# Three turned tiles that are turned again in the passes, from raw blocks, instead of being stored

## The reference

```python
h = relu(layernorm(x)); x = x + L0(h, adj)   # e = h with two small products; adj @ (adj.T @ e), normed, + h
h = relu(layernorm(x)); x = x + adj @ h                                    # pass 0
h = relu(layernorm(x)); x = x + chebyshev(h, adj, k = 3)                   # passes 1, 2, 3
h = relu(layernorm(x)); x = x + relu(d * ((adj + I) @ (d * (h @ W + b))))  # pass 4, d = (row sums + 1) ** -0.5
```

## Time and profile before

| | us |
|---|---|
| three runs | 1447.44, 1448.79, 1451.46 (median 1448.79) |
| profiled execution | 1448.4 |
| its span, first to last instruction | 1446.2 |
| turning stage, to the first product behind it | 551.4 |
| passes | 894.8 |

### The profile page before, as it was taken

The page is one execution under the profiler, slowest core; times in us unless marked ns, Lnnn a source line. Parts: engine busy times, 40 slices in busy tenths (PEclk is TensorE's granted clock), DMA queues, the critical chain, the costliest instruction groups (busy, mean ns, idle before and its releaser), DMA issues.

```text
span 1446.2 us, 18473 instructions
## 1 busy us (share of the span) xinstructions
PE 1419.2 (98%) x7601; PEld 600.5 (42%) x7601; DVE 491.8 (34%) x1082; ACT 399.3 (28%) x885; POOL 84.4 (6%) x67
## 2 busy tenths in 40 slices
PE   6999999999999999999999999999999999999998
PEld 3555555555555563333333333333333333333332
DVE  6694544544546533331132211011311121101044
ACT  2378778677776551000000000000000000000000
POOL 2210000000000038000000000000000000000000
PEclk9999999999999999999999999999999999999999
DMA  9999999999999998999996797899797948996998
GB/s 322 382 422 409 419 414 413 419 410 411 412 402 371 391 420 341 420 421 420 421 409 215 320 363 295 320 352 323 302 336 263 312 179 357 392 377 227 356 419 316
DMA packets 97607, 523.26 MB, mean 362 GB/s; under 512 B 18764, under 2 KB 18804, under 8 KB 54644
## 3 DMA queue, kind: packets, MB, share of 16 engines
q1 hardware_dynamic: 90436, 520.40, 91.4%
q10 hardware_dynamic: 7088, 1.67, 0.5%
HBM read 415.88 MB, written 106.17 MB: 361 GB/s over the span
## 4 chain that ended last, share of the span: by engine, by line
PE 78%; DMA 16%; ACT 3%; DVE 2%; POOL 1%; issue 1%; SPq 0%; ACTq 0%; POOLq 0%; DVEq 0%
PE turned L640 33%; PE acc L640 29%; DMA raw<-in_adj_dram 13%; PE t_acc L651 8%; PE turned L673 5%; ACT staged L882 3%; DMA over_wide<-adj_t 2%; PE turned L828 1%; DMA w_in<-in_L_gnn_W_i_dram 0%; PE t_rows L812 0%; PE turned L834 0%; DVE staged L1174 0%; PE acc L703 0%; ACT over_last L882 0%; PE t_acc L802 0%
## 5 line engine op out<-in xcount | busy, mean ns | idle before, releaser
L1134 DVE STREAM_TRANSPOSE staged<-raw 32x256 f32<-32x256 f32 x448 | 195.1, 435 | 5.8
L651 PE MATMUL t_acc<-raw,E 128*64 128x384 f32 (+1 forms) x1120 | 185.3, 478 | 5.1 <-DMA raw<-in_adj_dram 5.0
L882 ACT ACTIVATE staged<-turned 128x512 f32<-128x512 f32 x303 | 152.7, 636 | 104.1 <-PE turned L673 103.7
L926 ACT ACTIVATE t_t<-raw 128x768 uint8<-128x768 f32 (+1 forms) x216 | 177.2, 901 | 0.0
L640 PE MATMUL acc<-staged,t_cur 128*64 128x512 f32 x720 | 161.1, 596 | 0.0
L673 PE MATMUL turned<-ident,raw 128*128 128x128 f32 x1376 | 159.5, 274 | 0.0
L673 PEld LDWEIGHTS turned<-ident,raw 128*128 128x128 f32 x1376 | 149.8, 140 | 21.7 <-issue 21.7
L640 PE MATMUL turned<-over_last,C 128*64 128x512 f32 x672 | 152.1, 592 | 0.0
L651 PEld LDWEIGHTS t_acc<-raw,E 128*64 128x64 f32 x1120 | 78.4, 138 | 109.3 <-issue 85.7
L1277 POOL TENSOR_TENSOR rstd<-rstd,minus_half 128x8 f32<-128x8 f32 (+1 forms) x30 | 44.2, 1475 | 1265.9 <-DVE rstd L1036 1265.9
L640 PE MATMUL turned<-over_last,R 128*64 128x512 f32 x512 | 116.5, 593 | 0.0
(11 more groups left out here) (139 smaller groups left out, 1061.9 us busy)
## 6 DMA issues: line engine op xcount, KB each, us to landing
over_last<-adj_t SPq DMA_DIRECT2D x181, 1024.0 KB, 9.1
staged<-adj_t SPq DMA_DIRECT2D x91, 1024.0 KB, 9.4
raw<-in_adj_dram SPq DMA_DIRECT2D x60, 1536.0 KB, 19.5
adj_t<-staged SPq DMA_DIRECT2D x30, 3072.0 KB, 18.0
over_wide<-adj_t SPq DMA_DIRECT2D x23, 1024.0 KB, 7.7
raw<-in_adj_dram SPq DMA_DIRECT2D x10, 1024.0 KB, 15.0
adj_t<-over_last SPq DMA_DIRECT2D x8, 1024.0 KB, 14.9
adj_t<-C SPq DMA_DIRECT2D x2, 1024.0 KB, 21.7
```

The source lines that it names most:

```text
L651: last = nc.tensor.matmul(t_acc[h * D:(h + 1) * D, 0:columns], E[:, m * SUB + a, :], raw_of(g, m)[:, a, h * columns:(h + 1) * columns], st ...
L882: nc.scalar.activation(turned_into(g, u)[:, i * B:(i + 1) * B], turned[n % TURN_BANKS][:, :], ACT.Copy) \
L926: nc.scalar.activation(passed[n % 2][:, 0:chunks(g) * P], raw_of(g, m)[:, a, :], ACT.Copy, accum_out=deg_part[:, m * SUB + a, g:g + 1]).th ...
L1134: last = nc.vector.transpose(dst[b * SQ:(b + 1) * SQ, :, :, q * SQ:(q + 1) * SQ], src[q * SQ:(q + 1) * SQ, :, :, c * P + b * SQ:c * P + (b ...
```

## The change

Three tiles, (2,11), (3,14) and (4,8), the last third of the stored pairs (3,2), (4,3) and (2,4) (group, row), are no longer stored: those stores write 4096 words per partition instead of 6144 and no longer wait for the chunk that VectorE turns. In the passes these tiles are used nine times. Each time SP loads their raw blocks from `adj` into slot 0 (`room_raw`), in four DMAs of 256 KiB whose runs in DRAM are 128 words (512 B), and VectorE turns them into the tile's slot with 16 transposes of 32x512 (`turn_room`), in four quarters that stand at the end of steps chosen by `place_turning`. The number of loads from `adj_t` falls from 295 to 286. Slot 0 takes no turned tiles from step 28 until the last of the nine is used, at step 263. SP issues the raw blocks ahead of a load in its order and waits there until the room is turned.

```diff
+UNSTORED = [(2, 11), (3, 14), (4, 8)]
+QUARTERS = 4
+BUSY_BEHIND = [(1, 2, 3, 4, 7, 8, 9), (1, 2, 3), (1, 2, 3), (1, 2, 3, 4, 6), (1, 2)]
+ROOM_LANDS, ROOM_AHEAD = 6, 8
+ROOM_FROM = 28
...
+                no_room = n > last_raw or n in self.step_tile and self.step_tile.index(n) < ROOM_FROM
+                place = min((x for x in empty if no_room or x[1] != 0), key=lambda x: x[0])
...
+    def place_turning(self):
...
+        row_ends = {s + i for s, r in self.ended.items() for i in BUSY_BEHIND[self.rows[r][0]]}
...
+        for n in self.turned_no:
+            free = step_of[self.slot_before[n]][-1]
+            asked = max(end + 1, free - ROOM_AHEAD, step_of[self.room_after][-1] + 1)
+            after = next(x for x in self.loads if self.slot_before[x] is not None and step_of[self.slot_before[x]][-1] >= asked)
+            self.rooms_before.setdefault(after, []).append(n)
+            s = max(free + 1, end + 1)
+            while sum(products[asked:s]) < ROOM_LANDS:
+                s += 1
+            for q in range(QUARTERS):
+                while s in row_ends:
+                    s += 1
+                self.quarters_in.setdefault(s, []).append((n, q))
...
+                if (m, (g + 1) * CHUNKS // 2 - 1) in UNSTORED:
+                    words = STAGE_WORDS - TILE_WORDS
+                    sp.wait_ge(chunk_copied, COPIED_NO[g, m, words // B - 1])
...
+                sp.dma_start(adj_t[m, :, at:at + words], staged_pair(g, m)[:, 0:words]).then_inc(stored_by(g, 2 * m)[0], 16)
...
+            def load_room(n):
+                p, m, k, dual = plan.tiles[n]
+                if plan.turned_no[n] > 1:
+                    sp.wait_ge(room_turned, plan.turned_no[n] - 1)
+                else:
+                    sp.wait_ge(multiplied, plan.used_no(plan.room_after))
+                for c in range(2):
+                    for h in range(2):
+                        at = (2 * c + h) * SUB
+                        sp.dma_start(room_raw[:, at:at + SUB, :],
+                                     pair_v[:, m, h, :, (2 * k + c) * P:(2 * k + c + 1) * P]).then_inc(room_in, 16)
...
+            def turn_room(n, q):
+                if q == 0:
+                    dve.wait_ge(room_in, 64 * plan.turned_no[n])
+                    dve.wait_ge(multiplied, plan.used_no(plan.slot_before[n]))
+                tile = whole[plan.slot[n]].rearrange("p (b n) -> p b n", n=P)
+                for b in range(4):
+                    last = nc.vector.transpose(tile[b * SQ:(b + 1) * SQ, :, q * SQ:(q + 1) * SQ],
+                                               room_raw[q * SQ:(q + 1) * SQ, :, b * SQ:(b + 1) * SQ])
+                if q == QUARTERS - 1:
+                    last.then_inc(room_turned, 1)
```

More of the change, by code:

```diff
@@ L200, in __init__ @@
         loads_of = {}
+        self.turned_no = {}
+        last_raw = max(n for n in range(len(self.tiles)) if n not in self.slot and self.tiles[n][1:3] in UNSTORED)
         for n in range(len(self.tiles)):
             if n not in self.slot:
-                place = min(empty, key=lambda x: x[0])
+                no_room = n > last_raw or n in self.step_tile and self.step_tile.index(n) < ROOM_FROM
+                place = min((x for x in empty if no_room or x[1] != 0), key=lambda x: x[0])
                 empty.remove(place)
@@ L205, in __init__ @@
                 _, j, self.slot_before[n] = place
-                loads_of[j] = loads_of.get(j, 0) + 1
-                self.slot[n], self.load_no[n] = j, loads_of[j]
-                self.loads.append(n)
+                self.slot[n] = j
+                if self.tiles[n][1:3] in UNSTORED:
+                    self.turned_no[n] = len(self.turned_no) + 1
+                else:
+                    loads_of[j] = loads_of.get(j, 0) + 1
+                    self.load_no[n] = loads_of[j]
+                    self.loads.append(n)
@@ L209, in __init__ @@
+                if j == 0 and n < last_raw:
+                    self.room_after = n
                 if j != ONCE:
                     empty.append((self.used_no(n), j, n))
+                if n == last_raw:
+                    empty = [x for x in empty if x[1] != 0] + [(self.used_no(n), 0, n)]
+        self.place_turning()
+    def place_turning(self):
+        step_of = {}
+        for s, n in enumerate(self.step_tile):
+            for x in [n] * (n is not None) + self.duals_in.get(s, []):
+                step_of.setdefault(x, []).append(s)
+        products = [(n is not None) + len(self.duals_in.get(s, [])) for s, n in enumerate(self.step_tile)]
+        row_ends = {s + i for s, r in self.ended.items() for i in BUSY_BEHIND[self.rows[r][0]]}
+        self.rooms_before, self.quarters_in, end = {}, {}, 0
+        for n in self.turned_no:
[10 more added lines that the diff above has]
+                self.quarters_in.setdefault(s, []).append((n, q))
+                end = s
+                s += 1
+            assert end < step_of[n][0], (self.tiles[n], end, step_of[n])
@@ L629, in _ @@
             for n in plan.loads[len(AT_START):]:
+                for x in plan.rooms_before.get(n, []):
+                    load_room(x)
                 sp.wait_ge(multiplied, plan.used_no(plan.slot_before[n]))
@@ L1254, in _ @@
                         turn_squares(r)
+                for n, q in plan.quarters_in.get(s, []):
+                    turn_room(n, q)
         @block.gpsimd
```

18 lines of the change are left out of this document (14 added, 4 removed).

## The result

The changed kernel takes 1458.84 us (median of four runs, 1456.94 to 1463.3); the kernel before took 1449.65 beside it. The ratio is 1.0068, with a 95% interval of 1.0047 to 1.0088: slower by some 10 us. I had forecast 1452.4 and a range up to 1457. The profiled execution, 1456.94 with a span of 1455.1, is the shortest of the four; that of the kernel before took 1448.4.

What follows compares the result with a forecast made beforehand. TensorE, busy 98% of the span, was taken as the bound, with full transfer queues holding it back early. Terms -6.9 + 2.8 + 1.3 + 1.2 + 1.8 + 3.4 = +3.6 on 1448.8 gave 1452.4 us; 80% range 1445 to 1457.

Steps and rivals of the forecast that it cites:

- The stage: Turning stage ahead of the passes: three shorter stores save 7.5 us of transfers, and the passes start 6.9 us earlier.
- The first raw load: Loaded ahead of step 35's tile, where the queue is full: takes 3.4 us, makes TensorE wait at step 39, +2.8 us.
- The rival of dear packets: First rival: a raw load costs 5.4 us, steps 39 and 54 lose more, total 1455.6 us; chance 0.2.
- The squares: VectorE's nine transpose blocks in the passes, 11.4 us each; the first, at steps 36 to 39, costs +1.3 us.
- the fourth block: Steps 109 to 112, before row (1,4) ends: 11.4 us in a gap of 9.55, 1.9 late, +1.8 us.
- the seventh's own wait: Steps 220 to 223, before row (3,4) ends: gap of 7.24 us, 4.2 late, 0.8 of slack, +3.4 us.
- the third: Third block, tile (4,8) of pass 0: 1.9 us late, some 0.7 absorbed by TensorE's second batch, +1.2 us.
- The five blocks forecast at nothing: The other five VectorE blocks, including the second and sixth, end before the next row does: 0 us.
- The rival of short blocks: Second rival: transposes take 9.3 us a tile, so most blocks fit their gaps, total 1446.0 us; chance 0.2.
- The rival of the halved stage saving: Third rival: turning, issue and landing hold TensorE back, not bytes; half the 6.9 us is lost, 1455.9; chance 0.1.
- the first and third rival: Raw loads at 5.4 us (1455.6, chance 0.2) and half the stage's saving lost (1455.9, chance 0.1).
- the forecast's neighbourhood: Total time of 1449 to 1455 us around the forecast of 1452.4; chance 0.5.

Runs made afterwards that it cites:

- the stores alone: Kernel before with only the three stores shortened, no raw loads or turning by VectorE, neighbour tiles read instead: 1445.95 us, ratio 0.9968.
- the eight stores: Kernel before with eight short stores alone, at pairs 9, 11, 13, 15, 17, 19, 21 and 23, neighbour tiles read: 1439.11 us, ratio 0.9921.
- the plain load: Changed kernel with each raw block's four 512-byte-run transfers replaced by one load of the neighbour's stored tile in 8-KiB runs: 1458.41 us, ratio 1.0061.
- without the turning: Changed kernel with 15 of the 16 transposes of each tile left out, waits, raw loads and short stores kept: 1449.90 us, ratio 0.9996.
- the kernel with 18 transposes: Changed kernel with the first two transposes of the fourth use (steps 109 to 112) done twice: mean of two runs 1463.79 us.
- three early: Kernel before with three short stores alone, at pairs 9, 10 and 11, neighbour tiles read: 1443.57 us, ratio 0.9955.
- three late stores: Kernel before with three short stores alone, at pairs 22, 23 and 24, neighbour tiles read: 1442.90 us, ratio 0.9947.

## Why the prediction was wrong

By the profiled executions the forecast was +3.6 and the shift is +8.9, 5.3 us off.

**The stage: 2.3 us, the term most mis-sized.** "TensorE can take only what it waited ... So the passes start 6.9 us earlier." It is 4.6 in this trace, 1.7 to 5.3 (3.5 in the mean) in the eight traces with this stage, and 4.6 (2.8 to 6.5) by the ratio of the stores alone. The mechanism was right: the eight stores show TensorE's own pace as the floor, and what it can take is what it waited for. The step that failed is that each saving would be turned into time one for one as long as waiting lay behind it. In the changed kernel's trace TensorE waits for raw blocks again at pairs 21 to 23 (15.16, 15.40, 15.38 where 14.98, once 15.31, is its own), although two stores, 5.1 us of transfers, have gone by then and only 2.3 have been taken, and it waits 1.6 us more in the last pairs of the stage. The landing of the odd raw block tells the same: from 21.5 us after its issue it falls to 19.8 behind the first short store and to 19.4 behind the second, and is back at 21.6 three pairs later. Where the rest of the saving goes isn't shown. A smaller slip is that the 6.9 us of waiting were split wrongly over the stores: in the trace of before 0.9 of them lie between the first and the second and 2.2 between the second and the third, not 2.2 and 1.3; the sum doesn't change by it.

**The first raw load: 0.8 us.** The price of the packets was right: 3.4 forecast; the landings around it in the new trace are 610.8 and 614.3, 3.5 apart, and the plain load is 1.0 to 1.5 cheaper. The 0.6 us by which I let the transfers enter the passes ahead of TensorE was not there (the loads ahead of the raw one land 4.3 us earlier than before, where TensorE is 4.5 earlier), and so the whole load was paid for. The rule of the Trainium skill that I had weighed (page "DMA: Bandwidth & Descriptors", section "Specifications"), by which runs of 512 B are enough for line rate, does not hold for this load (3.5 us against 2.5). The rival of dear packets (5.4) falls too.

**The squares.** 11.44 us a block against 11.4: right to the tenth, and with it the fourth block (1.9 and 1.8) and the seventh's own wait (3.3 and 3.4). That the first comes to 1.3 as forecast is luck: its stop is 1.7, and 0.4 came back between steps 39 and 46, as it does without the turning (+0.57 to +0.14). For the third I had let 0.7 us be absorbed by TensorE's second batch; only 0.2 was: 1.7 in place of 1.2. The five blocks forecast at nothing cost nothing. The rival of short blocks falls.

**The clock: 1.7 us, a term that was missing.** I priced a stop of TensorE at its length. The seventh block's stop brought the clock from its upper level (2.4 GHz, granted clock 1.00) down to the lower (1.2 GHz, 0.50 in a row of the kernel with 18 transposes) for some microseconds. The trace of before could not price it, having in the passes up to 1440 us no stop of TensorE over 0.3 us, but the direction was to be had. The Trainium skill says, on the page "TensorE: Matmul & The Clock Gate" in the section "HAM oscillation — how this bites in real kernels", that a wait for a transfer can put TensorE back to its lower clock. The runs agree (behind waits of 2.0 and 2.9 us for a tile), and show it behind a stop of 1.8 us for VectorE too, shorter than the waits of the page's case.

The rival of the halved stage saving (1455.9, chance 0.1) named the right place: two thirds of the 6.9 came. Its reason, that the cycle of issue and landing and not the bytes holds TensorE back, is refuted by the kernels with eight, three early and three late stores, in which fewer bytes alone bring the pairs to TensorE's own pace.

The chances don't add up as said: the first and third rival and a third of the forecast's neighbourhood are 0.47 for slower, not 0.41, which leaves 0.39 for within. The measured time lies beyond the range's upper end, which none of the three rivals reached: two terms missed in the same direction, the stage and the clock, make up 4.0 of the 5.3 us.

## What to carry to other kernels

Work put on an idle engine is free only up to the moment at which that engine's next work is due for the critical one: 68 us of transposes cost nothing in the gaps, while a block 4 us too long for its gap cost 5 (3.3 of waiting and 1.7 of low clock). Read for each gap both ends, when the data and the target are free (not when the transfer lands alone) and when the engine's next work is due; and price a stop of TensorE of some 2 us and more at its length and, where the clock falls as it did here, 1.5 to 3 us on top. A transfer brought forward into a stretch with no slack costs its whole time there, whatever it spares later (2.3 us of 2.5 for the plain load, 3.7 for the raw blocks). One taken out gives less than its transfer time: three of 2.6 us each gave 7.7 us (5.5 to 9.9) at the stage's end, but 4.6 (2.8 to 6.5) and 4.2 (2.9 to 5.7) in its middle.

## What the runs showed of the hardware

- SP's queue stood for 15.7 us over the issue of four DMAs of 256 KiB in 512-byte runs while the queues were full (0.4, 5.1, 9.0 and 1.2 us each); for a plain load of the same size there the issue took 0.32. In the full queue (DMA share 1.01 and 1.02) that stop cost nothing that shows; the raw blocks landed 3.5 us behind the load ahead of them, the plain one 2.5.
- TensorE's granted clock fell behind stops as short as 1.8 us and stayed up behind others of 2.1, for a cost of 1.5 to 3.1 us where it fell (step 35 aside). A stop of 13.0 us cost 2.2 on top, no more than one of 3.2.
- VectorE's 32x512 fp32 transpose takes 703 ns, 32x256 435 and 32x128 303: a straight line in the elements.
